# First products of a routed mixture: another order of tiles, ScalarE copying two parts' weights, VectorE's routing placed tile by tile

## What is computed

```
dw1, dw2, dw3 = route(x_addr @ U1.T), route(x_addr @ U2.T), route(x_addr @ U3.T)   # top 3 of 12, softmax
h = sum_e dw1[:, e] * (x @ W1[e].T)        # 256 -> 1024
h = gelu(h)
y = sum_e dw2[:, e] * (h @ W2[e].T)        # 1024 -> 256
x = x + y + dw3 @ b2
```

## Time and profile before

| | us |
|---|---|
| median of 3 runs | 1117.47 |
| lowest, highest | 1114.49, 1118.03 |
| profiled execution | 1119.37 |
| its span | 1117.5 |
| PE busy in the span | 1047.1 (94%) |
| DVE busy | 664.2 (59%) |
| ACT busy | 378.0 (34%) |

### The profile page before, as it was taken

One profiled execution on the slowest core, in us unless ns is written; L12 is line 12 of the kernel. 1 busy time (PEld: TensorE's weight loads), 2 busy tenths in 40 slices (PEclk: granted clock), 3 DMA queues, 4 the chain that ended last, 5 costly groups with the idle time before them and its releaser, 6 DMA issues. The chain is left out here.

```text
span 1117.5 us, 20134 instructions
## 1 busy us (share of the span) xinstructions
PE 1047.1 (94%) x6560; PEld 753.3 (67%) x6560; DVE 664.2 (59%) x1541; ACT 378.0 (34%) x737; POOL 286.4 (26%) x306
## 2 busy tenths in 40 slices
PE   7999999999999999999998999798798999899996
PEld 3788854688999888788863443232236877577785
DVE  3988857776444544677767776767630266633612
ACT  0566644422111221566522333232222222122230
POOL 1221110000112000111013222154533577454431
PEclk8999999999899999999999999899989999999998
DMA  7000050000698000920022444279789999675634
GB/s 226 2 1 0 1 186 1 1 1 1 213 349 295 15 0 0 360 100 0 1 83 83 178 163 171 97 254 349 276 310 389 418 326 341 239 254 151 221 122 165
DMA packets 72057, 177.17 MB, mean 159 GB/s; under 512 B 10605, under 2 KB 31071, under 8 KB 70444
## 3 DMA queue, kind: packets, MB, share of 16 engines
q1 hardware_dynamic: 47362, 102.09, 24.9%
q0 software_dynamic: 20896, 69.75, 18.6%
q10 hardware_dynamic: 3722, 4.33, 1.2%
HBM read 126.06 MB, written 47.97 MB: 156 GB/s over the span
## 5 line engine op out<-in xcount | busy, mean ns | idle before, releaser
L2125 PE MATMUL f_psH<-W,f_xTk 128*128 (+2 forms) x216 | 106.0, 637 | 15.6 <-DVE f_stage L2300 14.6
L2224 ACT ACTIVATE shared<-f_psH 128x512 f32<-128x512 f32 x108 | 63.5, 597 | 153.1 <-PE f_psH L2125 128.4
L2174 PE MATMUL f_psT<-W,sel 128*64 (+2 forms) x432 | 100.5, 387 | 0.5 <-issue 0.5
L2174 PE MATMUL f_psT<-W,f_xg 128*128 (+1 forms) x432 | 97.8, 380 | 1.5 <-DVE shared L2447 1.5
L2125 PE MATMUL f_psH<-W,ctxT 128*128 (+2 forms) x216 | 98.8, 600 | 0.3 <-issue 0.3
L2447 DVE COPY shared<-f_psT 128x256 f32<-128x256 f32 x54 | 22.7, 422 | 125.4 <-PE f_psT L2174 100.0
L1903 POOL DMA_INDIRECT f_xg<-xn_d,f_toks x54 | 57.4, 1064 | 132.0 <-PE f_psT L2105 103.3
L2174 PEld LDWEIGHTS f_psT<-W,f_xg 128*128 128x128 f32 (+1 forms) x432 | 79.2, 188 | 12.2 <-issue 1.7
L2174 PEld LDWEIGHTS f_psT<-W,sel 128*64 128x64 f32 (+2 forms) x432 | 63.9, 153 | 26.8 <-issue 5.1
L2125 PEld LDWEIGHTS f_psH<-W,f_xTk 128*128 128x128 f32 (+2 forms) x216 | 33.5, 165 | 68.6 <-issue 68.6
L1903 POOL DMA_INDIRECT f_temps<-h_d,f_toks x54 | 52.8, 977 | 98.2 <-PE f_psH L2153 68.2
(11 more groups left out here) (338 smaller groups left out, 2246.6 us busy)
## 6 DMA issues: line engine op xcount, KB each, us to landing
p_d<-shared SPq DMA_DIRECT2D x54, 512.0 KB, 2.7
W<-in_f_W1T SPq DMA_DIRECT2D x12, 1024.0 KB, 17.3
W<-in_f_W2T SPq DMA_DIRECT2D x12, 1024.0 KB, 11.7
m_wg<-in_m_Wg SPq DMA_DIRECT2D x16, 512.0 KB, 4.2
m_wu<-in_m_Wu SPq DMA_DIRECT2D x16, 512.0 KB, 5.9
m_wd<-in_m_Wd SPq DMA_DIRECT2D x16, 512.0 KB, 6.2
h_d<-a_W SPq DMA_DIRECT2D x16, 512.0 KB, 6.3
f_g<-p_d SPq DMA_DIRECT2D x8, 384.0 KB, 5.4
```

What stands on the lines that cost most here:

```text
L2125: mm = pe.matmul(psH[at, n % 2, c, :], xTk[n % 2][:, k, at], weights, start=k == 0, stop=k == KD - 1)
L2174: mm = pe.matmul(psT[at, n % 2, 0:D], hT[n % 2][:, k, at], weights, start=k == 0, stop=k == KH - 1)
L2224: act.activation(po[:, n % 2, c * HH:(c + 1) * HH], psH[:, n % 2, c, :], ACT.Copy).then_inc(po_ready, 1)
```

## The change

The order of the first products is now one batch after the other, with the mixed tiles at the slots of `MIXED_AT`. VectorE copies only the second part's weights (4 per mixed tile, 72 in all); ScalarE copies the third and fourth part's of the six quarter tiles (8 each, 48 in all), in the section of `stage_section` and the one before, behind that section's products, with a semaphore of its own. VectorE goes through all slots from 0 with the routing spread over them. `pick` for the second and third routing takes both batches at once, in another half of `hot`; the exponentials and shares of all routings are taken once. The slots of the counts, list additions and sums are new: sums of batch 0 from slot 31 to 48, two or three slots apart. On SP the sum's store now comes ahead of the tile's. W2's expert 0 is loaded at slot 49. Nothing before the first products and nothing in the second ones is written otherwise, but for the index of the semaphore on the copies.

```diff
-                def pick(dve, one, r, h, b):
-
-                    lo, hi = batch(b)
-                    z, eq, least = Z[:, r, lo:hi], tmp[:, 0], first[:, :]
+                def pick(dve, one, r, h, lo, hi):
+
+                    n = hi - lo
...
+                MIXED_AT = (4, 7, 10, 12, 15, 18, 20, 23, 26, 28, 30, 33, 35, 38, 40, 43, 45, 48)
 
                 def first_order():
 
-                    out = [(0, i) for i in range(PLAIN)]
-                    behind = 0
-                    for j, i in enumerate(mixed):
-                        out.append((0, i))
-                        if j % 2 and j < MIX:
-                            out.append((1, behind))
-                            behind += 1
-                    for i in mixed:
-                        out += [(1, i), (1, behind)]
-                        behind += 1
-                    out += [(1, i) for i in range(behind, PLAIN)]
+                    out = []
+                    for b in range(B):
+                        plain, parts = iter(range(PLAIN)), iter(mixed)
+                        out += [(b, next(parts if b * TB + i in MIXED_AT else plain)) for i in range(TB)]
                     assert sorted(out) == [(b, i) for b in range(B) for i in range(TB)]
...
+                by_scalar = [u for u in uses if not u.second and u.group > 1]
+                scalar_at = {u: j for j, u in enumerate(by_scalar)}
+                vector_at = {u: j for j, u in enumerate(u for u in uses if u not in scalar_at)}
 
                 def staged(second, n, s, q):
                     return use_at[Use(second, n, s, q)]
 
+                def stage_section(n):
+
+                    last = [uses[j - STAGES] for j, u in enumerate(uses) if not u.second and u.slot == n and j >= STAGES]
+                    return max(0, min(n - 1, max([n - 2] + [u.slot + 1 for u in last])))
+
+                FIRST_MIXED = [n for n in range(LT) if F_ORDER[n][1] >= PLAIN]
...
-                    COUNTS_AT = (1, 11, 21)
-                    ADDS_AT = ((5, 6), (14, 15), (24, 26))
-                    EXP_AT, DWT_AT, BIAS_AT, DIAG_AT = (17, 43), 46, 2, S_MIXED + 2
-                    SUMS_AT, RESULTS_AT = (34, 8), TB + 11
+                    COUNTS_AT = (1, 12, 22)
+                    ADDS_AT = ((6, 9), (16, 19), (27, 30))
+                    EXP_AT, DWT_AT, BIAS_AT, DIAG_AT = 14, 37, 2, S_MIXED + 2
+                    SUMS_AT, RESULTS_AT = (31, 33, 36, 38, 41, 43, 46, 48), TB + 11
 
                     def sum_at(u):
-                        return SUMS_AT[u // NT] + 2 * (u % NT)
+                        return SUMS_AT[u] if u < NT else NT + 2 * (u % NT)
...
-                                if n == TB - MIX:
+                                if n == TB:
...
-                                            pe.wait_ge(stage_ready, staged(False, n, s, m - 1) + 1)
+                                            pe.wait_ge(stage_ready, vector_at[Use(False, n, s, 1)] + 1)
+                                        if m > 2:
+                                            pe.wait_ge(act_stage_ready, scalar_at[Use(False, n, s, m - 1)] + 1)
...
+                            def part_places(n, steps):
+                                b, i = F_ORDER[n]
+                                if 0 in steps:
+                                    act.wait_ge(owner_ready, b + 1)
+                                    others[n] = [act.value_load(owner_of(0, b, i, q), min_val=0, max_val=E1 - 1)
+                                                 for q in range(2, groups(i))]
+                                for s in steps:
+                                    c, k = divmod(s, KD)
+                                    for q in range(2, groups(i)):
+                                        j = staged(False, n, s, q)
+                                        if j >= STAGES:
+                                            u = uses[j - STAGES]
+                                            act.wait_ge(h_mm, 2 * u.slot + u.step // KD + 1)
+                                        act.activation(stage[:, j % STAGES, :], W1[:, others[n][q - 2], k, c * HH:(c + 1) * HH],
+                                                       ACT.Copy).then_inc(act_stage_ready, 1)
...
+                                for m in FIRST_MIXED:
+                                    if groups(F_ORDER[m][1]) > 2:
+                                        if n == stage_section(m) - 1:
+                                            part_places(m, range(STEPS // 2))
+                                        if n == stage_section(m):
+                                            part_places(m, range(STEPS // 2, STEPS))
+                                if n == EXP_AT:
+                                    act.wait_ge(gap_ready, 1)
+                                    flat = wt[:, :, :, :].rearrange("p r k t -> p (r k t)")
+                                    act.activation(flat, flat, ACT.Exp).then_inc(exp_ready, 1)
...
+                                e = dve.value_load(owner_of(0, b, i, 1), min_val=0, max_val=E1 - 1)
                                 for s in range(STEPS):
                                     c, k = divmod(s, KD)
-                                    for q in range(1, groups(i)):
-                                        j = staged(False, n, s, q)
-                                        if j >= STAGES:
-                                            u = uses[j - STAGES]
-                                            dve.wait_ge(h_mm, 2 * u.slot + u.step // KD + 1)
-                                        dve.tensor_copy(stage[:, j % STAGES, :], W1[:, e[q - 1], k, c * HH:(c + 1) * HH]
-                                                        ).then_inc(stage_ready, 1)
+                                    j = staged(False, n, s, 1)
+                                    if j >= STAGES:
+                                        u = uses[j - STAGES]
+                                        dve.wait_ge(h_mm, 2 * u.slot + u.step // KD + 1)
+                                    dve.tensor_copy(stage[:, j % STAGES, :], W1[:, e, k, c * HH:(c + 1) * HH]
+                                                    ).then_inc(stage_ready, 1)
...
+                            for n in range(LT):
+                                for m in FIRST_MIXED:
+                                    if n == (0 if m == FIRST_MIXED[0] else stage_section(m)):
+                                        stage_first(m)
+                                if n == 0:
+                                    pick(dve, one, 1, 1, 0, TT)
+                                if n == 1:
+                                    dve.wait_ge(count_mm, 2)
+                                    lists(dve, one, psN, 0, 1)
+                                    product_rows(dve, one, 1)
+                                if n == 4:
+                                    half_match(0, 0)
+                                if n == 7:
+                                    half_match(0, 1)
+                                if n == 8:
+                                    all_owners(0, 1)
+                                if n == 9:
+                                    pick(dve, one, 2, 0, 0, TT)
+                                    gaps()
+                                if n == 11:
+                                    found(0, 0, 1)
+                                    next_list(0)
+                                if n == 13:
+                                    dve.wait_ge(count_mm, 3)
+                                    lists(dve, one, psN, 1, 0)
+                                if n == 15:
+                                    half_match(1, 0)
+                                if n == 17:
+                                    half_match(1, 1)
+                                if n == 18:
+                                    all_owners(1, 0)
+                                if n == 20:
+                                    found(1, 1, 0)
+                                    next_list(1)
+                                    dve.wait_ge(exp_ready, 1)
+                                    shares()
+                                if n == 23:
                                     dve.wait_ge(count_mm, 4)
-                                    lists(dve, one, psN, 1)
-                                if n == PLAIN + 5:
-                                    for i in range(NT // 2):
-                                        match(2, i)
-                                if n == PLAIN + 7:
-                                    for i in range(NT // 2, NT):
-                                        match(2, i)
-                                if n == PLAIN + 9:
-                                    dve.wait_ge(at_used, 4 * NT)
-                                    found_tokens(dve, one, 1, 1, psF)
-                                    dve.sem_inc(list_ready, 1)
-                                    owners(dve, one, 1, 1)
-                                if n == PLAIN + 11:
```

(82 more changed lines are left out.)

65 lines of the change are left out of this document (17 added, 48 removed).

## The result

The changed kernel took 1090.5 us (median of 4 runs, 1087.9 to 1093.5) against 1117.8 for the kernel before in the same measurements; the ratio is 0.9762 (95% interval 0.973 to 0.980). Once more, beside three experiments, it was 0.9758 (0.973 to 0.979). The forecast was 1088.0.

The account below looks back on a forecast made before the run. The prediction took TensorE's first products to be held by waits for VectorE, which comes late rather than being full. 33.5 - 7 + 3 = 29.5 us saved gave 1088.0 us, range 1080 to 1101.

Parts of the forecast that it names:

- The floor: First products after tile 0: without waits and low clock they end at 807.2 instead of 840.6 us, 33.5 us to win.
- VectorE late, not full: First products: VectorE, busy 158.7 of 240.8 us, reaches some tiles late behind long pieces; TensorE waited 14.6 and 7.1 us.
- Tile 12: The tight place in the first products: VectorE arrives at 646.4 to 649.4 us, TensorE at 647.0; wait taken 1.5 us.
- ScalarE's copies: 48 weight copies in the first products, 0.49 us each, make tokens late at slots 40 and 48: 5 us, 0 to 8.
- The step that failed: First products beyond slot 12: VectorE's pieces are shorter than the sections between them; list waits of 7.1 us go.
- rival B: Half comes back as first-product DMA and ScalarE waits, gathers landing at 10.8 us: 18.5 us gained, 1099; chance 0.24.
- A: The forecast itself: VectorE in time for nearly all tiles, 1080 to 1094 us; chance 0.68.
- The gathers: Gathers for batch 0's sums land in 7.6 us, 10.8 at worst; earlier GpSimd issues, 0 to 3 us, left out.
- The DMA engines: Stretch of batch 0's sums, slots 29 to 50: 68 to 74 us of DMA work in 79, nearly full, not over.
- The border: Start of second products: ScalarE's first hidden tile binds, 3.2 us behind the first products' end against 6.5; 3 us taken.
- Rival C: Slower: on SP a late sum's store delays tile stores, ScalarE and TensorE; 3.7 us per sum eats the gain; chance 0.05.
- The sum: 33.5 us of waits and low clock, minus 7 of new waits, plus 3 where second products begin: 29.5 us saved.

## Why the prediction was right

- *The floor.* The stretch took 215.0 us for a floor of 207.0: 8.0 us of new waits and low clock, forecast 7. Of them 5.4 are idle, 1.7 are low clock at tile 40, and 0.9 I can give no place. The two traces of the kernel with both groups of copies moved come within 2.0 and 2.6 us of the floor, counted from the end of their own tile 0. So 33.5 us was the right size of what there was to win.
- *VectorE late, not full.* The kernel with the copies moved ahead shows it at tiles 35 and 40, where the same work in another order cut the wait from 3.0 to 0.8 us. The kernel with all copies on VectorE gains 14 us with VectorE busy for two thirds of the stretch. No run took work from VectorE at a place where no tile waited, so that it pays only ahead of late tiles is argued, not shown.
- *Tile 12.* Forecast at 646.4 to 649.4 us with a wait of 0 to 2.5; its first copy began at 647.1 and TensorE did not wait, where I had 1.5. The picks were 0.358 us an operation, 0.36 assumed. The experiment with the picks apart shows that it was as tight as said.
- *ScalarE's copies.* 0.52 us apart (four take 2.19), 0.49 assumed. Their cost on the path was over-sized: 2.2 us of late tokens against 5. In this trace it arises where it was placed, behind four copies in the stretch where ScalarE waits for stores, but in one section of tile 48 fully and one in part.
- *The step that failed:* in the forecast VectorE was in time for all tiles behind 12; tiles 35 and 40 came only in rival B. They waited 0.99 and 1.99 us, tile 40 with a fall of the clock behind it, and 1.9 and 3.3 us of waits stand at the same two tiles in the second trace of the kernel (the 3.3 for ScalarE's copy of a product, not for VectorE). The cause at these tiles is B's, the copies behind a sum; its size is 4.7 us (3.0 of waits, 1.7 of low clock) of B's 8. So a mixture of A and B happened, and that the total came out is in part luck: 5 for ScalarE was 2.8 too high and 1.5 for tile 12 was 1.5 too high, about as much as 0 for these tiles was too low (4.7).
- *The gathers* landed as before (median 7.8 us, longest 11.0), not at the worst value throughout as B needs. The 0 to 3 us that were set beside the sum for GpSimd's issues, should fewer copies on VectorE shorten them, are not borne out: an issue took 1.22 us on average before and 1.09 after, but 1.02 with all copies back on VectorE, and 1.18 in the old order with ScalarE's copies.
- *The DMA engines.* The working has a slip: with three sums in 30 us a sum costs 5.3 us, not 4.8, and the sums' stretch is then full, 78 of 79 us. Measured from 715 to 805 us the engines are at 0.94.
- *The border.* 2.1 us, forecast 3. The bound was named rightly (ScalarE's first hidden tile), but ahead of it stand its last two product copies, which end at 817.4 us, and that I had left out.
- *Rival C.* Did not occur; with sums two slots later a loss of that kind did, at 2 to 3 us per sum rather than 3.7, and only a third of it by the new order on SP.
- *The sum.* First products 25.4 us sooner (forecast 26.5), border 2.1 (3), the rest 0.6 (0): 28.2 us of the span for 29.5.

## What to carry to other kernels

An engine that is 60% busy can still be what the busiest one waits for: write down, for each tile that needs it, the length of what stands ahead in its list, and compare that with when the tile is reached. Then shorten or move only the pieces ahead of late tiles. A wait on a slow transfer belongs behind the work that others need next, and copies belong where their engine already idles: two moved blocks gave 7.7 us more here, on top of the 27 of the larger rewrite.

## What was not expected

- Two traces of the same kernel differ in where it waits: at tile 40 VectorE's copy was late by 1.99 us in one, and in the other ScalarE's product copy by 3.32. Here a single trace fixed the tile of a wait, but neither its size nor the engine behind it.
- The clock: behind a wait of 1.87 us at tile 35 matmuls ran on at 0.64 us, behind 1.99 at tile 40 they went to 1.06 from the third on, and behind 3.64 in the kernel with the picks apart at once to 1.11. The granted clock from 740 to 770 us, around tile 40, was 0.94. Where the lower of the two levels followed a wait, the mixed tile behind it took 1.4 to 2.9 us more than the 3.6 it takes otherwise.
- The kernel before took 1130.6 us in one group and 1119 in the others, a difference of 1%, nearly as large as one of the two parts of this change. The traces of that group have it in the second products. Its cause is open.
